# One written order of all steps per kind of batch, and a written PSUM buffer for each use, in place of slots and a planner, in an adaptive-layernorm transformer layer

## The reference

```
h = _layernorm(x) * (1 + ca) + sa
x = x + ga * attn(h, w_qkv, w_o)          # softmax over keys up to the query, scale 1/16
h = _layernorm(x) * (1 + cb) + sb
shared = silu(h @ w1.T) * (h @ w2.T) @ w3.T
scores = sigmoid(h @ router_w.T);  top 2 of scores + expert_bias
routed = sum over the two experts of score * ((silu(h1) * h2) @ w3[e].T)
x = x + gb * (shared + routed)
```

## Time and profile before

| | |
|---|---|
| median of 3 runs | 2179.09 us (2168.48 to 2185.64) |
| span of the profiled execution | 2187.9 us (no other time of it is given) |
| TensorE busy | 1958.7 us, 90% |
| VectorE busy | 1634.5 us, 75% |
| ScalarE busy | 1085.8 us, 50% |
| GpSimd busy | 830.9 us, 38% |
| mean granted TensorE clock | 0.951 of full speed |

### The profile page before, as it was taken

One profiled execution on the slowest core, in us unless ns is written; L12 is line 12 of the kernel. 1 busy time (PEld: TensorE's weight loads), 2 busy tenths in 40 slices (PEclk: granted clock), 3 DMA queues, 4 the chain that ended last, 5 costly groups with the idle time before them and its releaser, 6 DMA issues.

```text
span 2187.9 us, 47736 instructions
## 1 busy us (share of the span) xinstructions
PE 1958.7 (90%) x17942; PEld 1036.3 (47%) x17942; DVE 1634.5 (75%) x4447; ACT 1085.8 (50%) x1417; POOL 830.9 (38%) x825
## 2 busy tenths in 40 slices
PE   5778889899999989999999999999998988999995
PEld 2223334344444444444443434343434577788773
DVE  7887788777877788778878877878787376655575
ACT  1556445554555455545554555455554545444431
POOL 1121133234323432343233333333232357876653
PEclk7688879999999999999999999999998999999998
DMA  3346220201111201120211020211100446797696
GB/s 125 94 169 192 89 64 16 59 22 46 45 38 43 71 20 47 37 70 16 65 30 62 22 65 22 71 30 53 49 26 25 158 88 113 133 170 123 153 285 201
DMA packets 109663, 175.67 MB, mean 80 GB/s; under 512 B 14576, under 2 KB 80376, under 8 KB 108288
## 3 DMA queue, kind: packets, MB, share of 16 engines
q1 hardware_dynamic: 82656, 136.37, 20.9%
q0 software_dynamic: 26592, 36.00, 9.1%
q10 hardware_dynamic: 192, 0.26, 0.1%
HBM read 76.43 MB, written 70.44 MB: 67 GB/s over the span
## 4 chain that ended last, share of the span: by engine, by line
PE 55%; DVE 29%; ACT 5%; issue 4%; DMA 3%; POOL 2%; SPq 2%; POOLq 0%; ACTq 0%; DVEq 0%
PE bank L1841 11%; DVE bank L1279 8%; PE bank L1893 8%; DVE max_part L1273 8%; PE bank L1873 6%; PE bank L1804 5%; PE misc L1827 5%; PE bank L1780 4%; PE pv L1827 3%; PE bank L1754 3%; PE bank L1884 2%; PE bank L1920 2%; ACT arena L1076 2%; PE bank L1742 1%; DVE max_part L1279 1%
## 5 line engine op out<-in xcount | busy, mean ns | idle before, releaser
L1076 ACT ACTIVATE arena<-bank 128x1024 f32<-128x1024 f32 (+1 forms) x640 | 593.2, 935 | 422.7 <-PE bank L1804 419.1
L1279 DVE CUSTOM_DVE_ANT_0 bank<-bank,mask 128x512 f32<-128x512 f32 (+3 forms) x1024 | 472.2, 521 | 65.8 <-PE bank L1780 62.4
L890 POOL TENSOR_SCALAR_AFFINE_SELECT arena<-arena 128x512 f32<-128x512 f32 x256 | 170.3, 672 | 651.0 <-ACT arena L1076 650.4
L1841 PE MATMUL bank<-feat_parts,ffn_sb 128*128 128x512 f16 x1536 | 367.4, 388 | 8.8 <-DVE max_part L1279 4.9
L1273 DVE TENSOR_REDUCE max_part<-bank 128x2 f32<-128x1024 f32 x256 | 312.4, 1220 | 28.2 <-PE bank L1780 26.2
L1804 PE MATMUL bank<-arena 50*128 50x256 f16 (+1 forms) x2560 | 246.3, 272 | 68.7 <-DVE max_part L1273 22.7
L1780 PE MATMUL bank<-arena 48*128 48x512 f16 (+3 forms) x1536 | 234.1, 350 | 56.7 <-DVE max_part L1279 20.8
L953 POOL DMA_INDIRECT sum<-arena,feat x142 | 231.9, 1633 | 138.1 <-issue 67.0
L959 POOL TENSOR_TENSOR hidden<-silu_h,hidden 128x512 f16<-128x512 f32 x128 | 155.8, 1220 | 234.0 <-ACT hidden L1109 233.4
L1827 PE MATMUL misc<-arena,v_sb 128*32 128x256 f32 (+1 forms) x3072 | 239.8, 386 | 1.9 <-POOL arena L890 1.9
L1841 PEld LDWEIGHTS bank<-feat_parts,ffn_sb 128*128 128x128 f16 x1536 | 141.5, 99 | 197.8 <-issue 33.1
(11 more groups left out here) (218 smaller groups left out, 2477.2 us busy)
## 6 DMA issues: line engine op xcount, KB each, us to landing
arena<-parts SPq DMA_DIRECT2D x380, 64.0 KB, 2.3
feat<-lists SPq DMA_DIRECT2D x71, 265.0 KB
sum<-feat_parts SPq DMA_DIRECT2D x9, 1024.0 KB, 6.1
rows<-x SPq DMA_DIRECT2D x8, 1024.0 KB, 5.5
x_sb<-x SPq DMA_DIRECT2D x16, 512.0 KB, 5.6
sum<-norm SPq DMA_DIRECT2D x14, 512.0 KB, 3.3
ffn_parts<-hidden SPq DMA_DIRECT2D x8, 768.0 KB, 4.1
arena<-ffn_parts SPq DMA_DIRECT2D x8, 768.0 KB, 6.7
```

Source lines behind the costliest of these rows:

```text
L890: gp.affine_select(p, p, [[0, GH], [1, P]], ALU.is_ge, 0.0, 0, -1).then_inc(masked, 1)
L1076: sc.activation(to[:, :, lo:QC], of[:, :, lo:QC], ACT.Exp, scale=SCALE / QK_SCALE ** 2).then_inc(exp_done, 1)
L1279: last = vec.tensor_tensor_reduce(scored, scored, mask[:, 512 - nk:], scale=1.0, scalar=NEG, op0=ALU.add, op1=ALU.max, accum_out=max_part[ ...
L1841: last = mm(to[:, 512 * m:512 * m + 512], w_up[s][W_PART[i]][:, f, m * RH + h * P:m * RH + (h + 1) * P], feat_parts[:, A_PART[i], f, c * 5 ...
```

## The change

`work(v)`, its tables, and `buffers(v, was)` with its planned durations go. In their place stand two tables of text. `ORDER_OF[v]` is the whole list of steps in its order, `BANK_OF[v]` one digit for each use of a PSUM buffer, in the order in which the uses begin. The steps of each list are the same as before, in another order: two `scores` can follow each other, values no longer keep a fixed distance, an `up` or `down` can be split around other steps. The list of `start` is unchanged. The last user of each buffer is now followed through all batches in turn. The diff, cut to the begin of `first`, all of `loop`, the late part of `end`, the buffers of `loop`, and the code:

```diff
-def work(v):
...
-WORK = {v: work(v) for v in BODY}
+WORK = {v: listed(ORDER_OF[v]) for v in BODY}
...
+ORDER_OF = {
+    "first": """
+        max:1:0 max:1:1 share:0 share:1 qk:2 scores:0 max:1:2 scores:1 scores:2 max:1:3 max:1:4 scores:3 values:0 values:1 max:1:5
+        scores:4 max:1:6 zero:0 raw:0 scores:5 max:1:7 turn_out:0 max:1:8 values:2 values:3 values:4 values:5 raw:1 max:1:9 max:1:10 normalise:0 share:2
+        scores:6 scores:7 scores:8 scores:9 scores:10 max:1:11 values:6 max:1:12 max:1:13 max:1:14 max:1:15 max:1:16
...
+    "loop": """
+        scores:0 scores:1 max:1:0 values:-4 values:-3 max:1:1 max:1:2 scores:2 values:-2 values:-1 raw:-1 max:1:3 up:-2:0 up:-2:1 max:1:4 up:-2:2 up:-2:3
+        up:-2:4 scores:3 up:-2:5 turn_out:-1 scores:4 normalise:-1 values:0 max:1:5 scores:5 values:1 raw:0 max:1:6
+        scores:6 values:2 values:3 max:1:7 max:1:8 ot:0 turn_out:0 normalise:0 ot:1 max:1:9 values:4
+        scores:7 max:1:10 values:5 raw:1 values:6 scores:8 max:1:11 scores:9 values:7 scores:10 max:1:12
+        scores:11 values:8 values:9 max:1:13 max:1:14 op:0 up:-1:0 scores:12 rest:0 up:-1:1 up:-1:2 up:-1:3 up:-1:4 max:1:15
+        scores:13 turn_out:1 up:-1:5 values:10 values:11 raw:2 max:1:16 max:1:17 shifts:1 hid:-2 hid:-1 normalise:1 qk:2 turn_out:2 var:0
+        scores:14 down:-4:0 down:-4:1 down:-4:2 norm2:0:0 scores:15 scores:16 values:12 values:13 norm2:0:1 max_turn:1 values:14 values:15
+        scores:17 scores:18 down:-3:0 down:-3:1 down:-3:2 down:-2:0 down:-2:1 down:-2:2 max:2:0 halves:0 ln:0 low:0 down:-1:0 max:2:1 max:2:2 down:-1:1
+        down:-1:2 router:0 store:-1 scores:19 scores:20 scores:21 values:16 values:17 values:18 values:19 normalise:2
+        scores:22 scores:23 up:0:0 up:0:1 raw:3 up:0:2 route:0 rank:0 place:0 scatter:0 up:0:3 scores:24 up:0:4 up:0:5 turn_out:3 scatter:1 scatter:2
+        scores:25 max:2:3 values:20 values:21 raw:4 max:2:4 scores:26 hid:0 up:1:0 up:1:1 up:1:2 normalise:3 turn_out:4 normalise:4 up:1:3
+        scores:27 max:2:5 up:1:4 up:1:5 values:22 max:2:6 scores:28 max:2:7 values:23 values:24 max:2:8
+        scores:29 scatter:3 values:25 values:26 values:27 max:2:9 up:2:0 raw:5 turn_out:5 max:2:10 up:2:1 up:2:2 up:2:3 hid:1 up:2:4 max:2:11 up:2:5 up:3:0
+        up:3:1 up:3:2 max:2:12 up:3:3 scores:30 up:3:4 max:2:13 up:3:5 up:4:0 up:4:1 hid:2 up:4:2 max:2:14 up:4:3
+        scores:31 load_x1 up:4:4 up:4:5 load_x:1 max:2:15 normalise:5 scores:32 hid:3 hid:4 values:28 values:29 values:30 max:2:16 max:2:17 shifts:2 qk:3
+        scores:33 up:5:0 up:5:1 up:5:2 values:31 raw:6 spread1:0 scores:34 scores:35 up:5:3 turn_out:6 up:5:4 spread1:1 up:5:5 max_turn:2 up:6:0 up:6:1 up:6:2
+        up:6:3 up:6:4 normalise:6 up:6:5 scores:36 norm1 op:1 scores:37 scores:38 values:32 values:33 values:34
+        scores:39 rest:1 scores:40 max:3:0 values:35 values:36 max:3:1 scores:41 values:37 max:3:2
+        scores:42 values:38 values:39 hid:5 max:3:3 max:3:4 hid:6 up:7:0 raw:7 up:7:1 up:7:2 scores:43 up:7:3 turn_out:7 up:7:4 normalise:7 up:7:5
+        scores:44 max:3:5 values:40 values:41 hid:7 max:3:6 scores:45 values:42 raw:8 scores:46 max:3:7 values:43
+        scores:47 max:3:8 var:1 values:44 values:45 raw:9 scores:48 down:0:0 scores:49 max:3:9 down:0:1 down:0:2 max:3:10
+        scores:50 max:3:11 turn_out:8 normalise:8 turn_out:9 scores:51 turn:0 max:3:12 max:3:13 values:46 values:47 values:48 turn:1 norm2:1:0 max:3:14
+        down:1:0 down:1:1 down:1:2 max:3:15 scores:52 values:49 values:50 values:51 norm2:1:1 halves:1 max:3:16 max:3:17 qk:0 down:2:0 down:2:1 raw:10
+        normalise:9 scores:53 shifts:3 down:2:2 ln:1 low:1 turn_out:10 down:3:0 scores:54 scores:55 down:3:1 down:3:2
+        scores:56 max_turn:3 normalise:10 up:8:0 up:8:1 up:8:2 scores:57 scores:58 up:8:3 up:8:4 up:8:5 values:52 max:0:0
+        scores:59 values:53 max:0:1 scores:60 values:54 values:55 scores:61 scores:62 max:0:2 values:56 values:57 hid:8
+        scores:63 max:0:3 values:58 values:59 store:0 max:0:4 scores:64 values:60 values:61 max:0:5 max:0:6 up:9:0 up:9:1 up:9:2 raw:11 raw:12
+        scores:65 up:9:3 up:9:4 up:9:5 scores:66 max:0:7 scores:67 turn_out:11 normalise:11 turn_out:12
+        scores:68 scores:69 max:0:8 values:62 values:63 values:64 normalise:12 max:0:9 max:0:10 up:10:0 up:10:1 up:10:2 up:10:3
+        scores:70 up:10:4 load_gates up:10:5 max:0:11 scores:71 values:65 values:66 max:0:12 max:0:13 values:67 values:68 router:1 route:1 hid:9 qk:1
+        scores:72 v:0 scores:73 max:0:14 values:69 values:70 raw:13 max:0:15 scores:74 turn_out:13 normalise:13 up:11:0 up:11:1 hid:10 up:11:2 max:0:16
+        max:0:17 up:11:3 up:11:4 up:11:5 up:12:0 up:12:1 up:12:2 up:12:3 up:12:4 hid:11 up:12:5 hid:12 rank:1 place:1 scatter:4 scatter:5 shifts:0 v:1
+        scores:75 values:71 scatter:6 max_turn:0 values:72 values:73 scores:76 scores:77 raw:14 up:13:0 up:13:1 up:13:2 up:13:3
+        scores:78 scores:79 load_x:0 scatter:7 up:13:4 up:13:5 turn_out:14 values:74 values:75 hid:13 normalise:14
+    """,
...
+        tup:69 out_make:8 out_store:7 out_store:8 out_load:11 ty:68 tup:70 up:11:0 up:11:1 tlo:69 up:11:2 tlo:70 up:11:3 up:11:4 up:11:5 hid:11 out_make:9
+        ty:69 up:12:0 up:12:1 out_store:9 up:12:2 up:12:3 up:12:4 up:12:5 up:13:0 up:13:1 up:13:2 up:13:3 out_make:10 hid:12 out_store:10 up:13:4 up:13:5
+        hid:13 ty:70 up:14:0 up:14:1 up:14:2 up:14:3 up:14:4 up:14:5 up:15:0 hid:14 up:15:1 up:15:2 up:15:3 up:15:4 up:15:5 hid:15 down:4:0 down:4:1
+        out_make:11 down:4:2 down:5:0 down:5:1 down:5:2 down:6:0 out_store:11 down:6:1 down:6:2 down:7:0 down:7:1 first_loads own:0 down:7:2 own:1 out_end
...
+BANK_OF = {
+    "start": "0120120120120120120120120",
...
+    "loop": """
+        12012010212102010212012012012101220021201202101021020210102101012012120210120201010220012010202012021021012102210212012012120121012012021021
+        0212102121012102102120121021021021202102120120212101201201
+    """,
...
+def listed(text):
     out = []
...
+    for word in text.split():
+        kind, *at = word.split(":")
+        out.append((kind, *map(int, at)))
     return out
...
+RINGED = ("scores", "max", "up", "down", "op", "ot", "ln", "router", "turn", "qk", "v", "max_turn", "rank", "count", "mods", "xr", "tup", "ty")
 
 
 def use_of(step):
     return step[:3] if step[0] == "max" else step[:2]
 
 
-def buffers(v, was):
-
-    now, free, owner, took, after = 0, [0] * BUFFERS, list(was), {}, {}
-    closed = set(was)
-    for kind, *at in WORK[v]:
-        for of, reader in READER.items():
-            if reader == kind and (of, at[0]) in took:
-                free[took[(of, at[0])]] = now + READ[of]
-                closed.add((of, at[0]))
-        use = use_of((kind, *at))
-        if kind in RINGED and use not in took:
-            open_ = [i for i in range(BUFFERS) if owner[i] in closed]
-            i = min(open_, key=lambda i: (max(free[i], now), free[i], i))
-            if use in LAST_USES:
-                i = LAST_USES[use]
-                assert i in open_, use
-            now = max(now, free[i])
-            took[use], after[use], owner[i] = i, (owner[i], owner[i] in took), use
-        now += BUSY.get(kind, 0)
-        if kind in RINGED and kind not in READER and (kind not in PARTS_OF or at[1] == PARTS_OF[kind] - 1):
-            free[took[use]] = now + (READ_MASKED if kind == "max" and at[1] % NCH in MASKED else READ[kind])
-            closed.add(use)
-    return took, after, tuple(owner)
-
-
-USES, AFTER, LEFT = {}, {}, {None: (None,) * BUFFERS}
-BEFORE = {"start": None, "first": "start", "second": "first", "loop": "second", "last": "loop", "end": "last"}
-for v in BEFORE:
-    USES[v], AFTER[v], LEFT[v] = buffers(v, LEFT[BEFORE[v]])
-assert LEFT["loop"] == LEFT["second"]
+BATCHES = [(-1, "start"), (0, "first"), (1, "second")] + [(b, "loop") for b in range(2, B - 1)] + [(B - 1, "last"), (B, "end")]
+USES, AFTER = {}, {}
+owner = [None] * BUFFERS
+for b, v in BATCHES:
+    USES[v], AFTER[b] = {}, {}
+    banks = iter("".join(BANK_OF[v].split()))
+    for step in WORK[v]:
+        use = use_of(step)
+        if step[0] in RINGED and use not in USES[v]:
+            i = int(next(banks))
+            USES[v][use], AFTER[b][use], owner[i] = i, owner[i], (b, use)
+    assert next(banks, None) is None, v
 
 
...
             def take(b, v, use):
 
-                was, here = AFTER[v][use]
-                if was is not None:
-                    was_read(b if here else b - 1, was)
+                if AFTER[b][use] is not None:
+                    was_read(*AFTER[b][use])
                 return buffer_of(v, use)
```

More of the change, by code:

```diff
@@ L183 @@
-TABLES = {"first": (FIRST,), "second": (SECOND,), "loop": (SPILL, TAIL, HEAD, ALWAYS), "last": (SPILL_OF_LAST, TAIL_OF_LAST, LAST), "end": ()}
-TABLES = {v: tuple(by_slot(x) for x in tables) for v, tables in TABLES.items()}
-END_BEGIN = [
-    [("fetch", 4), ("fetch", 5), ("fetch", 6), ("fetch", 7)],
```

(9 more changed lines are left out.)

290 lines of the change are left out of this document (133 added, 157 removed).

## The result

The changed kernel takes 2034.4 us (four runs, 2031.7 to 2036.6) where the kernel before takes 2176.6 beside it: a ratio of 0.935 (interval 0.932 to 0.937), or 142 us less. 55 were forecast.

> The changed kernel as it is, on the chip of the three runs beside it, so that they can be set against it and not only against the kernel before: 0.935 of the time before, as the first time.

What follows compares the result with a forecast made beforehand. No engine is full: TensorE and VectorE take turns, TensorE mostly waiting for PSUM banks. 5 x (-9) - 8 - 2 + 3 - 3 = -55 us, from 2179 to 2124, taken as 2125; range 2085 to 2185.

Steps and rivals of the forecast that it cites:

- Step times: TensorE in a loop batch: start-to-start step times, such as scores 0.32 us and values 0.58, sum to 186 us.
- Banks, loop: PSUM bank uses in a loop batch: short covers fall from 22.6 to 3.6 us, by this term alone gaining 19.
- Balance, loop: Loop batch: summing the busier engine's work per stretch gives -9 us at the finer cut; with covers and clock -11.
- Rival (a): Whole kernel: bank covers decide and VectorE keeps up; -17 us per loop batch, -103 in all, 2076 us; chance 0.09.
- route: Loop batch: TensorE's 2.12 us stall at route:0 goes or shrinks below 1, the low clock with it; inside the -11.
- SP and stacking: Loop batch: new waits for DMA-stacked parts at max:2:0 and max:0:0, charged 2 us per batch, from nothing to 5.
- Batches 0, 1, last: The batches outside the loop, priced by stretches and covers: +3 us for batch 0, -2 for batch 1, -8 for last.
- End: Very end: hid:12 and hid:13 now precede ty:70's scatters on GpSimd, last hidden step 3 us earlier; -3 us.
- (b): Whole kernel: VectorE is the bound where it matters, so little is gained; 2167 us, within 1%; chance 0.14.
- (c): Stacking waits lower the clock in loop batches, batches 0 and 1 lose too; +35 us, 2214 us; chance 0.12.
- The signs: What would show it: loop batches about 204 us, bank waits for maxima roughly halved, VectorE's share above 82%.

Runs made afterwards that it cites:

- e4: The changed kernel with a tail of TensorE-only matmul patterns behind it, twelve turns of each, results unread; 2098.1 us in one run.
- e3: The kernel before with values of each even unit delayed to run in pairs with those of the next odd unit; 2250.3 us, ratio 1.033.
- e7: The kernel before with only values, raw, turn_out and normalise placed as in the changed kernel, buffers by the old planner; 2370.5 us, ratio 1.073.
- e8: The kernel before with up:0 one slot later, behind route, in the five loop batches, buffers replanned; 2226.1 us beside 2218.7, ratio 1.0033.
- e10: The changed kernel with small moves in batches 0, 1, loop and last, kept if a three-queue sum got shorter; 2129.1 us beside 2069.9.
- e1: The changed kernel's order with PSUM buffers chosen by the planner of before in place of the written ones; 2055.9 us, ratio 0.944.
- e6: The changed kernel with values and scores matmuls interleaved by halves at 141 places; 2148.9 us, ratio 0.969.

## Why the prediction was wrong

The sign was right and the size was not: 55 us were forecast and 142 measured. Between the two profiles, part by part, 55 us more than forecast came off in the loop, 23 in batch 1, 13 in batch 0 with the setup, 6 in the last and 3 at the end. By its own steps:

- **Step times (the start).** "a `scores` step is 0.32 us (965.34 to 965.66), a full `values` step 0.58", and so on, summed to 186 us and taken as constant on both sides. They hold one or two changes of layout each (e4: 0.22 and 0.43 bare). This is the step that failed first: from "no instruction is added or removed" I went to "nothing has a cost of its own", and that left out 518 changes of 0.12 us, 62 us in all, 7 per loop batch.
- **Banks, loop.** "By this term alone a loop batch gains 19 us": the measured gain is 20. But in the batch shown (21.0) 12.2 of it are busy time (7 layout, 1.6 the clock, the rest below) and 8.8 are idle time. The term's whole size was right by chance: of 22.6 us of short covers only 15.4 were idle time to begin with. e3 and e7 show that its direction is real.
- **Balance, loop.** This was the wrong choice. I preferred "at its finer cut" -9 to the covers' -19, since VectorE stood at 9.70 of 10 us. After the change both engines are full in the same windows, so most of the turns that they took belonged to the old order and were no bound. VectorE's queue didn't vanish: the longest wait that is left in a loop batch, 2.97 of 6.6 idle us, stands behind it. Rival (a), to which I gave 0.09, was nearest: it said -17 per loop batch and -6 at the end, and was still 40 us short.
- **route.** The wait is gone, as forecast. But e8, which takes it out of the old order (with 92 other banks), gains nothing: a loop batch of it still has 17.9 us of idle time, mostly in waits for other banks, and more of its work runs at the lower clock than before. So the stall by itself isn't shown to have carried any of the -11. The half clock behind it was priced at 3.3 us per loop batch; the change gave back about half, since 3.4 us at 0.50 now stand behind the new wait of 2.97 us, where 6.8 us stood behind the old one. As to the Trainium skill ("TensorE: Matmul & The Clock Gate", section "Loop structure matters more than you think"), by which VectorE's copies don't break warmth: waits for VectorE of 2.12 us and, after the change, of 2.97 us are both followed by a clock of 0.50, so the trace doesn't agree. What the rule would make of the time, no run here isolates.
- **SP and stacking.** Charged 2 us per batch, measured 0.2 to 0.8. Covers of 12.4 to 14.3 us were nearly enough. That real time runs "some 8% longer than step times" was a slip: 213.5 against the 186 of its own count is 15%, which makes the covers longer. e10 has a longer one: 3.0 us.
- **Batches 0, 1, last.** Forecast +3, -2, -8; measured -15.8 (with the setup -9.8), -25.0, -13.9. Batch 0 and 1 have 63 and 67 fewer changes of layout (8 us each) and the last 94 (11 us), batch 1 went from a clock of 0.92 to 0.96 (some 8 us of its 194), and the written buffers of batch 0 and 1 gave 8 and 7 us (e1). Of batch 0 the prediction named the weights' DMAs and the clock, "which these counts don't hold", and then priced it by the counts.
- **End.** Forecast -3, measured -6.3: the two hidden steps come before the tile's scatters, and the last wait is 4.42 us, from 10.04, where I had said 7:

```profile
2005.50 12.31 PE L1854 MATMUL bank<-ffn_sb,hidden 128*128 128x256 f16 x96 [4.42 <-POOL hidden L921]
```

  Mechanism right, size off.
- **Rivals (b) and (c)** fell: VectorE didn't hold the time at 2167, and no stacking wait in a loop batch passed 0.7 us.
- **The signs.** Loop batches took 193 us where 204 were to show it. The waits of `scores` for maxima weren't halved: 3.5 us against 3.2, now nearly all in one wait; those of `max` for maxima went from 1.9 to nothing. VectorE's share of the span is 80%, not above 82. And the forecast's 0.65 with half of (a) and of (b) is 0.77, so the range left out more than "2 in 10".

The two profiled spans differ by 155 us. Of these, 66 are idle time that went, mostly bank waits, and 89 are busy time. Of the 89, 62 are layout changes (e4's price times the count). 19 are the clock, by the table above (84 to 65): 8 in batch 1, 8 in the loop, 6 in batch 0 with the setup, less 3 from there on. And 310 waits over 0.15 us became 170. A `scores` step is recorded for 0.39 us where the next begins after 0.32; before a wait those 0.07 us count as busy, which makes some 10 us, an estimate. Together that is 91, as near to 89 as such prices can be. Not every wait is followed by a low clock, and to which of them its part is owed stays open.

## What to carry over

Time the steps of TensorE by their neighbours, not only by themselves: where steps of different tile shapes alternate, count the changes, since they are work that no instruction count shows. Before you compare busy times, see how much of each ran at the lower clock: it can hide such a price, as in e3 and e7. Work that needs no PSUM buffer is the filler between uses that do; group it where a bank is being read, and move the rest with it, or it turns into waits. And a sum that fits two orders within 2 us need not fit a third: once a search uses it, what it leaves out (DMAs, clock) can decide.

## What the runs showed of the hardware

- A change between row tiles, column tiles and the full array on TensorE costs 0.11 to 0.12 us (0.21 to 0.24 there and back), from `max` to `scores`, both row tiles, nothing (e4). In place it is about 0.125, over eleven executions (the table).
- Half of a `values` step, its matmuls into two of the four groups of 32 columns, takes as long as the whole step into all four (0.56 and 0.58 us, each with its change of layout; e6).
- Waits of TensorE for VectorE of 2.12 us (before) and 2.97 us (after) are each followed by a granted clock of 0.50; in the loop batches of e1, where no wait passes 0.95 us, the clock is 1.00.
- The same two programs run 1.6 and 1.7% slower on one chip than on another (2212.3 and 2176.6; 2069.9 and 2034.4), with the ratio unchanged. In a loop batch of the changed kernel this is 1.6 us of busy and 4.7 us of idle time of TensorE. Part of the idle time stands behind a stretch of 2.67 us near the first exponentials of the next batch, in which ScalarE waits for nothing that the profile shows in the program, and TensorE then 1.75 us for ScalarE.
